# Block attention with a ternary feed-forward: chunk 5's feed-forward begun two steps sooner, a new order for chunks 6 and 7, ternary weights a step later

## The chip, the cores and the metric

One Trainium2 chip, one core. The metric is the device time of one execution in microseconds (us); the kernel before has a median of 299.28 us over three runs.

## What is computed

Input x is (2, 1024, 128) in float32. Sixteen heads of 64 attend in blocks of 16 tokens: each block of queries sees its own block, the two before it and the first token (later tokens are masked), and after the softmax the heads are mixed with a 16x16 matrix. Then comes a feed-forward of 512 hidden units with ternary weights, and a layer norm behind each of the two. Cut to what matters:

```python
qkv = xp @ w_qkv                                   # 128 -> 3 * 1024
sim = einsum('bhnid,bhnjd->bhnij', qw * scale, kw) # 16 queries x (1 + 5 * 16) keys, masked
attn = einsum('gh,bhnij->bgnij', w_th, softmax(sim))
out = concat(out_bos, einsum('bhnij,bhnjd->bhnid', attn, vw)) @ w_out + b_out
x = layernorm(x + out)

alpha = mean(abs(w)); w_t = sign(w) * (abs(w) > 0.5 * alpha)   # both weights
h = gelu((x / (rms(x) + 1e-8)) @ w_up_t.T)                     # 128 -> 512
y = (h / (rms(h) + 1e-8)) @ w_down_t.T                         # 512 -> 128
x = layernorm(x + y)
```

## The kernel before, in words

The engines' programs are written out by hand, one function for each engine, with semaphores between them; every engine works its own list in order. The 2048 tokens are 8 chunks of 256. The main loop has 32 steps, four to a chunk; a step handles four blocks of 16 queries. "s_c" below is the step a piece of data belongs to.

- `scores(s)`: 64 small matmuls and a mask on PE into bank 0. `shift(s)`: VectorE takes the maximum (L751) and subtracts it (L753). ScalarE's Exp (L632). `total(s)`: VectorE's sum (L759) and reciprocal (L761). `normalise(s)`: POOL (L448).
- Two steps later (LAG 2): `transposes` of the probabilities (L1025), which `at_hi` on ScalarE and `at_lo` on VectorE (L744) turn into the high and low part AT; `c_part` (L1064), 12 matmuls of the probabilities with windows of x; one step on, `ct_hi` on ScalarE and `ct_lo` on VectorE (L739) split its result into CTh and CTl. Float32 accuracy is had from two fp32r parts everywhere: high part, low part, and `split3` (L922 to L924) with three matmuls.
- `y_part`: 12 matmuls a step that prepare the next chunk's queries (bank 2 and 3, copied by ScalarE as Yb in `y_out`); they end with step 27. In step s%4=0 the scores wait for all Yb of their chunk.
- `o_part(n, p)`: the output projection of chunk n in four blocks of 12 matmuls, one block a step from step 4n+6 on, for chunk 6 two blocks in each of steps 30 and 31, for chunk 7 in the end.
- The feed-forward of chunk n starts at step 10+4n (F_LAG) and takes a phase k a step: k=0 `stage` (ScalarE, bias, attnS, L586), `attn_back` (PE transposes), `residual` (VectorE L767 to L778: sum, statistics), `variance_roots` (POOL L454); k=1 `up_input` (VectorE L783 to L791), `x1_T` (PE L1091), `layernorm` (VectorE L796); k=2 `x1_hi` (ScalarE), `x1_lo` (VectorE L801), `up(n,0)` (PE L1101, L1102), `gelu(n,0)` (ScalarE L603); k=3 `up(n,1)`, `gelu(n,1)`, `hidden_high` (VectorE L807, gTh), `hidden_low` (POOL L461, gTl), `squares` (POOL L467, L469), `down` (PE L1110, L1111); in the next chunk's k=0 `down_out` (ScalarE, dS), `down_back` (PE: transposes L1119 and 16 one-column sums of squares L1123), `hidden_sum` (VectorE L818), `hidden_root` (POOL L474), `second` (VectorE L823 to L841), `last_root` (POOL L480), and in its k=1 `result` (VectorE L847). Then SP stores.

A helper says which phase runs: `divmod(s - F_LAG, 4)`, one chunk at a time. So chunk 5's phases 0 and 1 fall in steps 30 and 31 and everything from its `x1_hi` on stands in the list behind the loop, mixed with chunks 6 and 7. Chunk 7's projection there comes in pieces, its last block behind `down(6)`. The weights' preparation is done in the first steps: `fills` moves data through free banks, and `ternary()` (VectorE L730, L733), four instructions of 128x512, stands at the end of step 0; its results are transposed on PE in step 2 (fill "t"). PE's step 2 begins by waiting for the copies of fill ("x", 2).

The result tile y2 is one buffer; `second(n)` waits for the store of chunk n-1.

## Time and profile before

| | us |
|---|---|
| median of 3 runs | 299.28 |
| lowest, highest | 297.99, 300.93 |
| the profiled execution | 297.8 |
| its span, first to last instruction | 295.7 |
| PE busy / VectorE / ScalarE / POOL | 235.7 / 202.6 / 143.0 / 127.0 |
| mean granted TensorE clock | 0.895 |

The span is shorter than the execution's time by 2.1 us, which lie around it. The profile covers one execution. Times in the trace count from the start of the span. PE is TensorE, DVE is VectorE, ACT is ScalarE, POOL is GpSimd; "[0.53 <-DVE x1Tl L801]" behind a row means that the engine sat idle 0.53 us before it and what ended that. PEclk is the granted clock: 1.00 is 2.4 GHz, 0.50 is 1.2 GHz.

### The profile page before, as it was taken

The numbers are of one execution on the slowest core, as the hardware profiler recorded it, in microseconds if no ns is written. First come the engines' busy times: TensorE is split into PE (matmuls) and PEld (weight loads), VectorE is DVE, ScalarE is ACT, GpSimd is POOL, SyncE is SP. The second block draws the span as 40 slices with busy tenths as digits, with TensorE's granted clock in tenths as the row PEclk, the third lists the DMA queues.
The fourth block names the chain that finished last, engine by engine and source line by source line (L and its number), as shares of the span: only waits on it lengthen the run. The fifth ranks groups of instructions, "written<-read, shape, count | busy, mean of one in ns | idle before, by whom it ended". The sixth has DMA issues, their size and how long they took to land.

```text
span 295.7 us, 9352 instructions
## 1 busy us (share of the span) xinstructions
PE 235.7 (80%) x4002; PEld 208.8 (71%) x4002; DVE 202.6 (68%) x505; ACT 143.0 (48%) x264; POOL 127.0 (43%) x148
## 2 busy tenths in 40 slices
PE   2799399989999989889988999898879745953440
PEld 2699399879898968778877888787758624952320
DVE  0757668786688669867876886698758867154631
ACT  2474246755654854595368456844742531200200
POOL 6115124134234564474457535844564162073250
PEclk9999689999999999999999999999968955867555
DMA  7635800100100200020011001000000000000000
GB/s 255 163 111 173 211 5 11 48 2 9 51 21 2 58 2 21 14 60 2 20 43 35 4 19 50 26 22 20 0 2 21 20 18 0 2 0 18 19 0 19
DMA packets 18621, 11.65 MB, mean 39 GB/s; under 512 B 2004, under 2 KB 17940, under 8 KB 18452
## 3 DMA queue, kind: packets, MB, share of 16 engines
q1 hardware_dynamic: 18000, 10.01, 11.7%
q10 hardware_dynamic: 580, 1.05, 1.2%
q8 instruction: 31, 0.51, 0.8%
q14 instruction: 10, 0.08, 0.1%
HBM read 8.91 MB, written 2.10 MB: 37 GB/s over the span
## 4 chain that ended last, share of the span: by engine, by line
DVE 39%; PE 19%; issue 16%; POOL 12%; ACT 10%; DMA 2%; POOLq 0%; DVEq 0%; ACTq 0%
DVE CTl L739 8%; DVE E L753 5%; DVE mx L751 4%; POOL gT L467 4%; DVE AT L744 4%; ACT E L632 3%; POOL gT L469 3%; DVE sm L759 3%; PE bank L922 3%; PE bank L923 2%; PE bank L924 2%; ACT L603 2%; PE bank L1064 2%; PE bank L1041 2%; POOL gTl L461 2%
## 5 line engine op out<-in xcount | busy, mean ns | idle before, releaser
L448 POOL TENSOR_TENSOR E<-E,rc 128x400 f32<-128x400 f32 x32 | 27.6, 863 | 83.1 <-DVE rc L761 83.0
L523 ACT ACTIVATE Yb<-bank 128x512 f32<-128x512 f32 x64 | 38.0, 594 | 30.6 <-PE bank L924 30.2
L739 DVE TENSOR_TENSOR CTl<-bank,CTh 128x512 fp32r<-128x512 f32 x64 | 41.1, 683 | 15.2 <-ACT CTh L523 14.9
L523 ACT ACTIVATE CTh<-bank 128x512 fp32r<-128x512 f32 x64 | 34.7, 598 | 18.3 <-PE bank L1064 18.1
L922 PE MATMUL bank<-xTh,Gh 128*128 128x256 f32 x128 | 38.3, 299 | 1.2 <-ACT Gh L523 1.2
L922 PE MATMUL bank<-CTh,Mh 128*128 128x256 f32 x128 | 37.4, 293 | 0.9 <-DVE CTl L739 0.9
L632 ACT ACTIVATE E<-E 128x400 f32<-128x400 f32 x32 | 17.2, 538 | 41.6 <-DVE E L753 41.6
L923 PE MATMUL bank<-CTl,Mh 128*128 128x256 f32 x128 | 36.9, 288 | 0.0
L924 PE MATMUL bank<-CTh,Ml 128*128 128x256 f32 x128 | 36.9, 288 | 0.0
L924 PE MATMUL bank<-xTh,Gl 128*128 128x256 f32 x128 | 36.0, 281 | 0.0
L923 PE MATMUL bank<-xTl,Gh 128*128 128x256 f32 x128 | 36.0, 281 | 0.0
L1064 PE MATMUL bank<-AT,xw 50*128 50x256 f32 x384 | 33.1, 308 | 1.5 <-DVE AT L744 1.5
L1041 PE MATMUL bank<-xT,Yb 128*32 128x50 f32 x2048 | 30.6, 214 | 1.4 <-ACT Yb L523 1.4
L1041 PEld LDWEIGHTS bank<-xT,Yb 128*32 128x32 f32 x2048 | 26.2, 113 | 7.1 <-issue 7.0
L1064 PEld LDWEIGHTS bank<-AT,xw 50*128 50x128 f32 x384 | 26.4, 197 | 6.7 <-issue 2.6
L759 DVE TENSOR_REDUCE sm<-E 128x8 f32<-128x400 f32 x32 | 18.2, 569 | 16.9 <-ACT E L632 16.9
L1025 PE MATMUL bank<-ident,E 128*128 128x128 f32 x128 | 22.4, 300 | 4.6 <-issue 4.6
L922 PEld LDWEIGHTS bank<-CTh,Mh 128*128 128x128 f32 x128 | 25.2, 197 | 1.1 <-issue 1.0
L922 PEld LDWEIGHTS bank<-xTh,Gh 128*128 128x128 f32 x128 | 24.6, 192 | 1.6 <-ACT Gh L523 1.4
L923 PEld LDWEIGHTS bank<-CTl,Mh 128*128 128x128 f32 x128 | 25.2, 197 | 0.0
L924 PEld LDWEIGHTS bank<-CTh,Ml 128*128 128x128 f32 x128 | 25.0, 195 | 0.0
L923 PEld LDWEIGHTS bank<-xTl,Gh 128*128 128x128 f32 x128 | 24.4, 191 | 0.0
(132 smaller groups left out, 512.7 us busy)
## 6 DMA issues: line engine op xcount, KB each, us to landing
raw<-in_L_attn_x SPq DMA_DIRECT2D x36, 64.0 KB
w_sb<-in_L_attn_w_qkv ACTq DMA_DIRECT2D x2, 512.0 KB, 5.2
pt_rows<-PT SPq DMA_DIRECT2D x1, 1024.0 KB, 5.8
R<-pt_rows SPq DMA_DIRECT2D x1, 1024.0 KB, 4.9
xr<-in_L_attn_x SPq DMA_DIRECT2D x6, 128.0 KB
out<-y SPq DMA_DIRECT2D x6, 128.0 KB
raw<-in_L_attn_x SPq DMA_DIRECT2D x12, 56.0 KB
xq<-in_L_attn_x SPq DMA_DIRECT2D x2, 256.0 KB, 5.3
```

The lines of the kernel that those rows point to most:

```text
L448: tt(e, e, rc[s % 2][:, :].unsqueeze(2).broadcast_to([P, TILES, WIN]), ALU.mult).then_inc(s_norm, 1)
L523: copy = lambda o, i, **k: nc.scalar.activation(o, i, ACT.Copy, **k)
L632: nc.scalar.activation(e, e, ACT.Exp).then_inc(s_exp, 1)
L739: v.tensor_tensor(ct_view(CTl[s // 4 % 2], s % 4, q), c_view(q), ct_view(f32(CTh[s // 4 % 2][:, :, :]), s % 4, q), ALU.subtract).then_inc( ...
L753: v.tensor_tensor(E[k][:, :, 0:WIN], scores, mx[k][:, :].unsqueeze(2).broadcast_to([P, TILES, WIN]), ALU.subtract).then_inc(s_sub, 1)
L759: v.tensor_reduce(sm[k][:, :], E[k][:, :, 0:WIN], AX.X, ALU.add).then_inc(s_sum, 1)
L922: mm(o, wh, rh, start=start, stop=False, **k)
L923: mm(o, wh, rl, start=False, stop=False, **k)
L924: return mm(o, wl, rh, start=False, stop=stop, **k)
L1025: ins = nc.tensor.transpose(o[:, :, IL * f:IL * f + IL], E[s % 2][:, k:k + 2, :].rearrange("p t w -> p (t w)"), ident[:, :])
L1041: mm(bank[S_BANK][lo:lo + 32, WIN * tile:WIN * tile + WIN], Yb[s // 4 % 2][:, ytile, lo:lo + 32], keys, start=(tile == 0), stop=False, ski ...
L1064: ins.append(mm(bank[C_BANK[q]][:, col], xw[s // 4 % 2][row, m, c, :], AT[row, a, col], start=(n == 0), stop=(n == 2)))
```

## The change

- Chunk 5: its projection runs two blocks each in steps 26 and 27, its feed-forward starts at step 28 in place of 30, in banks 2 and 3, which y_part has left. Steps 28 to 31 then hold phases of two chunks. Its `down` and what follows stand in the end.
- `down_back` is split: the sums of squares become `square_sum` with a semaphore of their own. For chunks 6 and 7 they go to bank 7 and take the squares of all four hidden tiles (32 one-column sums), which ScalarE computes with Square into a new tile gsq; before, POOL squared and added.
- For chunk 6, gTh is copied by ScalarE and gTl computed by VectorE (before VectorE and POOL).
- y2, mv2 and rstd2 have two buffers, each store buffer its own semaphore.
- In every step PE does `up(n,0)` behind y_part (before ahead of it) and `down(n)` behind `c_part` (before ahead); in steps s%4=3 ScalarE copies the second Yb ahead of Exp (before behind).
- `ternary()` moves to the end of step 1, and PE's step 2 waits for the copies of the last "p" fill instead of ("x", 2).
- The end behind the loop is a new list on each engine, with chunk 7's projection ahead of `up(6)` and `down(6)`; `c_part(30)` writes banks 0 and 1.

```diff
+            gsq = last.enter_context(nc.sbuf_tensor("gsq", [P, FT, CHUNK], F32))
...
         def o_parts(s):
-            if s < 30:
+            if s < 26:
                 return [divmod(s - O_LAG, 4)] if s >= O_LAG else []
-            return [(6, 2 * (s - 30)), (6, 2 * (s - 30) + 1)]
+            return {26: [(5, 0), (5, 1)], 27: [(5, 2), (5, 3)], 30: [(6, 0), (6, 1)], 31: [(6, 2), (6, 3)]}.get(s, [])
         def ffn(s):
-            return divmod(s - F_LAG, 4) if s >= F_LAG else (-1, -1)
-        UP_BANK = {5: (1, 2), 6: (2, 3), 7: (5, 6)}
-        AT_BANK = {6: 0, 7: 4}
-        DN_BANK = {6: 0, 7: 4}
+            first = [F_LAG + 4 * n for n in range(5)] + [28]
+            return [(n, s - f) for n, f in enumerate(first) if 0 <= s - f < 6]
+        UP_BANK = {5: (2, 3), 6: (0, 1), 7: (5, 6)}
+        AT_BANK = {5: 2, 6: 3, 7: 4}
+        def ss_bank(n):
+            return bank[O_BANK] if n >= 6 else dn_bank(n)
+        def c_bank(s, q):
+            return bank[q if s == 30 else C_BANK[q]]
...
 # POOL, behind the loop
-            hidden_low(5, 0)
             variance_roots(6)
-            hidden_low(5, 1)
-            squares(5, 0)
-            squares(5, 1)
             hidden_root(5)
-            hidden_low(6, 0)
-            hidden_low(6, 1)
             last_root(5)
-            squares(6, 0)
-            squares(6, 1)
+            variance_roots(7)
             hidden_root(6)
-            variance_roots(7)
+            hidden_root(7)
             last_root(6)
-            squares(7, 0)
-            squares(7, 1)
-            hidden_root(7)
             last_root(7)
...
 # ScalarE
-                need(act, f_back, n if n < 6 else n - 1)
+                need(act, f_ss, {6: 0, 7: 6}.get(n, n))
+            def hidden_high(n, t):
+                copy(gTh[n == 6][:, o, :], gT[n == 6][:, o, :]).then_inc(f_gh, 1)
+            def squares(n, t):
+                need(act, f_ss, n)
+                nc.scalar.activation(gsq[:, o, :], gT[n == 6][:, o, :], ACT.Square).then_inc(f_sum, 1)
...
                 y_out(s, 0)
+                if s % 4 == 3:
+                    y_out(s, 1)
                 nc.scalar.activation(e, e, ACT.Exp).then_inc(s_exp, 1)
-                y_out(s, 1)
+                if s % 4 < 3:
+                    y_out(s, 1)
...
 # ScalarE, behind the loop, after the change:
+ at_hi(30), ct_hi(29), stage(6), at_hi(31), ct_hi(30), down_out(5), ct_hi(31), x1_hi(6), stage(7),
+ gelu(6,0), hidden_high(6,0), gelu(6,1), hidden_high(6,1), squares(6,0), squares(6,1), down_out(6),
+ x1_hi(7), gelu(7,0), gelu(7,1), squares(7,0), squares(7,1), down_out(7)
...
 # VectorE
-                if s == 0:
+                if s == 1:
                     ternary()
...
 # VectorE, behind the loop, after the change:
+ at_lo(30), ct_lo(29), at_lo(31), ct_lo(30), ct_lo(31), residual(6), hidden_sum(5), up_input(6),
+ layernorm(6), x1_lo(6), second(5), residual(7), hidden_low(6,0), hidden_low(6,1), result(5),
+ up_input(7), hidden_sum(6), x1_lo(7), layernorm(7), hidden_high(7,0), hidden_low(7,0),
+ hidden_high(7,1), hidden_low(7,1), second(6), hidden_sum(7), second(7), result(6), result(7)
...
 # PE
                 if s == LAG:
-                    pe.wait_ge(s_eva, read_no("A", "x", 2))
-                    pe.wait_ge(s_evd, read_no("D", "x", 2))
+                    pe.wait_ge(s_eva, read_no("A", "p", 2))
+                    pe.wait_ge(s_evd, read_no("D", "p", 3))
...
 # PE, behind the loop, after the change:
+ transposes(30), c_part(30), attn_back(6), transposes(31), down(5), c_part(31), down_back(5),
+ square_sum(5), o_part(7,0), o_part(7,1), o_part(7,2), x1_T(6), o_part(7,3), up(6,0), attn_back(7),
+ up(6,1), down(6), square_sum(6), down_back(6), x1_T(7), up(7,0), up(7,1), down(7), square_sum(7),
+ down_back(7)
```

## Rows read from the trace of the kernel before

**Rows 1.** Busy time by stretch: start:end, length, each engine's us (count), PEclk, DMA share, GB/s
```profile
core 0: us, PE busy (x) PEld busy (x) DVE busy (x) ACT busy (x) POOL busy (x), PEclk, DMA share, GB/s
180.00:200.00 20.00, 18.78 (x363) 16.73 (x363) 14.83 (x41) 13.46 (x25) 11.47 (x13) 1.00 0.13 36
240.00:250.00 10.00, 2.57 (x15) 1.95 (x16) 7.41 (x12) 1.17 (x4) 6.03 (x7) 0.50 0.02 6
270.00:280.00 10.00, 2.76 (x10) 2.07 (x10) 6.42 (x28) 1.58 (x3) 1.67 (x2) 0.57 0.05 14
```
**Rows 2.** The chain that ended last: start us, us, what
```profile
core 0 of [0], span 295.7 us
...
225.12 0.12 PE bank L922
...
277.75 0.21 PE bank L1102
```
**Rows 3.** Timeline, first loop steps: start, us, engine, line, operation, [idle before, releaser]
```profile
28.14 1.55 DVE L730 TENSOR_SCALAR tern<-w_ff,tsum 128x512 f32<-128x512 f32 x2
31.06 0.57 DVE L751 TENSOR_REDUCE mx<-bank 128x8 f32<-128x400 f32 x1
...
35.37 1.08 PE L1025 MATMUL bank<-ident,E 128*128 128x128 f32 x4 [4.61 <-issue]
...
37.12 0.69 DVE L744 TENSOR_TENSOR AT<-bank,AT 128x512 fp32r<-128x512 f32 x1 [1.78 <-ACT AT L523]
38.22 0.57 DVE L751 TENSOR_REDUCE mx<-bank 128x8 f32<-128x400 f32 x1 [0.41 <-PE bank L1047]
...
40.58 0.57 DVE L759 TENSOR_REDUCE sm<-E 128x8 f32<-128x400 f32 x1 [1.18 <-ACT E L632]
...
42.77 1.29 DVE L739 TENSOR_TENSOR CTl<-bank,CTh 128x512 fp32r<-128x512 f32 x2 [0.83 <-ACT CTh L523]
```
**Rows 4.** Timeline, steps 20 to 23, where the period is 27.9 us
```profile
150.16 0.38 PE L1101 MATMUL bank<-x1Th,wuT 128*128 128x256 f32 x1 [0.53 <-DVE x1Tl L801]
...
161.07 0.38 PE L1110 MATMUL bank<-gTh,wdT 128*128 128x256 f32 x1 [0.96 <-POOL gTl L461]
...
163.37 1.29 DVE L739 TENSOR_TENSOR CTl<-bank,CTh 128x512 fp32r<-128x512 f32 x2 [1.66 <-ACT CTh L523]
...
165.44 0.16 DVE L818 TENSOR_SCALAR hss<-bank 128x2 f32<-128x2 f32 x1 [0.18 <-PE bank L1123]
...
175.31 0.54 ACT L632 ACTIVATE E<-E 128x400 f32<-128x400 f32 x1 [2.79 <-DVE E L753]
```
**Rows 5.** Timeline, steps 26 to 31 and the first table load behind them
```profile
193.45 0.56 DVE L751 TENSOR_REDUCE mx<-bank 128x8 f32<-128x400 f32 x1
...
216.43 0.39 PE L1110 MATMUL bank<-gTh,wdT 128*128 128x256 f32 x1 [2.34 <-POOL gTl L461]
...
233.25 0.57 DVE L759 TENSOR_REDUCE sm<-E 128x8 f32<-128x400 f32 x1 [0.60 <-ACT E L632]
...
235.33 1.28 ACT L603 ACT_TABLE_LOAD   x1
236.62 1.08 ACT L603 ACTIVATE gT<-bank 128x512 f32<-128x512 f32 x2
```
**Rows 6.** Timeline behind the loop
```profile
241.34 1.26 POOL L461 TENSOR_TENSOR gTl<-gT,gTh 128x512 fp32r<-128x512 f32 x1
241.40 2.21 DVE L783 SCALAR_TENSOR_TENSOR rms<-roots,eps_rms 128x1 f32<-128x1 f32 x2 [2.12 <-POOL roots L454]
...
244.44 1.82 DVE L791 TENSOR_SCALAR x1n<-res,mv,rn 128x128 f32<-128x128 f32 x2
...
247.39 0.68 DVE L744 TENSOR_TENSOR AT<-bank,AT 128x512 fp32r<-128x512 f32 x1
...
250.43 1.29 DVE L739 TENSOR_TENSOR CTl<-bank,CTh 128x512 fp32r<-128x512 f32 x2 [1.53 <-ACT CTh L523]
...
267.21 0.47 ACT L586 ACTIVATE attnS<-bank,b_sb 128x255 f32<-128x255 f32 x1 [2.18 <-PE bank L924]
...
274.10 0.35 DVE L783 SCALAR_TENSOR_TENSOR rms<-roots,eps_rms 128x1 f32<-128x1 f32 x2 [1.12 <-POOL roots L454]
...
289.46 0.60 DVE L847 TENSOR_SCALAR y<-y,mv,rstd 128x128 f32<-128x128 f32 x2 [0.81 <-POOL rstd L480]
```

More of the change, by code:

```diff
@@ L112, in attention_ffn @@
         dS = sb("dS", [P, CHUNK])
-        y2 = sb("y2", [P, CT, P])
+        y2 = [sb(f"y2_{i}", [P, CT, P]) for i in range(2)]
         st = sb("st", [P, CT, 6])
@@ L565, in ct_hi @@
                     act.wait_ge(s_C, 2 * s + 1 + q)
-                    copy(ct_view(CTh[s // 4 % 2], s % 4, q), c_view(q)).then_inc(s_CTh, 1)
+                    copy(ct_view(CTh[s // 4 % 2], s % 4, q), c_view(s, q)).then_inc(s_CTh, 1)
             def at_hi(s):
@@ L613, in _ @@
             for s in range(STEPS):
[L614 to L620 removed]
+                for n, k in ffn(s):
+                    if k == 4:
+                        down_out(n)
+                    if k == 0:
+                        stage(n)
+                    if k == 2:
+                        x1_hi(n)
                 if s == LAG + 1:
@@ L656, in _ @@
             gelu(7, 1)
+            squares(7, 0)
+            squares(7, 1)
             down_out(7)
@@ L851, in _ @@
             for s in range(STEPS):
-                n, k = ffn(s)
-                if k == 1 and n > 0:
-                    result(n - 1)
-                if k == 2:
-                    x1_lo(n)
-                if k == 3:
-                    hidden_high(n, 0)
+                for n, k in ffn(s):
+                    if k == 5:
+                        result(n)
+                    if k == 2:
+                        x1_lo(n)
+                    if k == 3:
+                        hidden_high(n, 0)
                 if s == LAG + 1:
@@ L864, in _ @@
                     at_lo(s - LAG)
-                if k == 0 and n > 0:
-                    hidden_sum(n - 1)
-                if k == 1:
-                    up_input(n)
-                if k == 3:
-                    hidden_high(n, 1)
+                for n, k in ffn(s):
+                    if k == 4:
+                        hidden_sum(n)
+                    if k == 1:
+                        up_input(n)
+                    if k == 3:
+                        hidden_high(n, 1)
                 shift(s)
-                if k == 0 and n > 0:
-                    second(n - 1)
+                for n, k in ffn(s):
+                    if k == 4:
+                        second(n)
                 total(s)
@@ L911, in _ @@
             hidden_low(7, 1)
+            second(6)
             hidden_sum(7)
             second(7)
+            result(6)
             result(7)
@@ L1135, in _ @@
                 scores(s)
-                if k == 0 and n > 0:
-                    down_back(n - 1)
-                if k == 2:
-                    up(n, 0)
-                if k == 3:
-                    up(n, 1)
+                for n, k in ffn(s):
+                    if k == 4:
+                        down_back(n)
+                        square_sum(n)
+                    if k == 3:
+                        up(n, 1)
                 if s < STEPS - 4:
@@ L1155, in _ @@
                     o_part(*part)
-                if k == 0:
-                    attn_back(n)
-                if k == 1:
-                    x1_T(n)
-                if k == 3:
-                    down(n)
+                for n, k in ffn(s):
+                    if k == 0:
+                        if n == 5:
+                            pe.wait_ge(s_Ye, 64)
+                        attn_back(n)
+                    if k == 1:
+                        x1_T(n)
                 if s >= LAG:
                     c_part(s - LAG)
+                for n, k in ffn(s):
+                    if k == 3 and n < 5:
+                        down(n)
             transposes(30)
-            pe.wait_ge(s_Ye, 64)
-            up(5, 0)
-            up(5, 1)
-            pe.wait_ge(s_sub, STEPS)
+            c_part(30)
+            pe.wait_ge(f_gelu, 12)
             attn_back(6)
-            c_part(30)
             transposes(31)
-            x1_T(6)
+            down(5)
             c_part(31)
-            down(5)
-            up(6, 0)
-            up(6, 1)
+            down_back(5)
+            square_sum(5)
             o_part(7, 0)
             o_part(7, 1)
-            down_back(5)
             o_part(7, 2)
+            x1_T(6)
+            o_part(7, 3)
+            up(6, 0)
+            attn_back(7)
+            up(6, 1)
             down(6)
-            o_part(7, 3)
+            square_sum(6)
             down_back(6)
-            pe.wait_ge(s_ATl, STEPS)
-            attn_back(7)
             x1_T(7)
@@ L1190, in _ @@
             down(7)
+            square_sum(7)
             down_back(7)
```

189 lines of the change are left out of this document (101 added, 88 removed).

## The prediction, made blind

> **What bounds the kernel now.** I read the page's first line for the span, then the table of stretches, then the chain that ended last, then each engine's timeline at four places: the first loop steps, one steady period, steps 26 to 31, and everything behind the loop. The table [rows 1] tells the two halves apart. In a steady stretch TensorE is busy 18.8 of 20 us at a granted clock of 1.00, and VectorE 14.8. Behind the loop, from 240 to 250 us, TensorE is busy 2.6 of 10 us at 0.50, and between 270 and 280 us 2.8 of 10 at 0.57, while no other engine is full. A fifth of the span [rows 2] is a serial tail: chunks 6 and 7 hand small pieces from engine to engine. So a microsecond of work matters in the loop only where a wait closes the loop, and in the tail nearly everything on the chain counts. By the chain a 256-column matmul costs 0.12 us from start to start at 2.4 GHz (clock 1.00) and 0.21 at 1.2 GHz (0.50) [rows 2].
>
> **Part 1, ternary a step later.** The four ternary instructions take 2.9 us of VectorE (28.14 to 31.1), and the maximum of step 1 starts only behind them at 31.06, though its scores were done by 28. What follows hangs on it: PE's first transposes at 35.37 had stood idle 4.61 us, the first AT waited 1.78, the first CTl starts at 42.77 [rows 3]. After the change VectorE runs the maximum at 28.2, the exponentials' sum to 30.7, the copies of xT to 32.4, the ternary work until 35.3 and then AT at once, because the transposes no longer wait for the third xT fill (only for the banks of "p") and start near 30.7. The work is the same; VectorE's waits go: 1.78 (AT), 0.41 (maximum), about 0.6 of the sum's 1.18 and 0.6 of CTl's 0.83 [rows 3]. Sum 3.4 us. Bounds: 0 if the ternary group lands on an equally tight place, 4.6 if PE's whole idle time goes. PE must wait for the ternary weights until 35.3, hidden by y_part until about 34.2. From there to step 6 the loop is a VectorE/ScalarE cycle, so I keep **-3.4**.
>
> **Part 2, order inside the steady loop.** PE's two largest waits in one period are 0.53 (x1Tl) and 0.96 (gTl) [rows 4]. The second Yb copy of a step s%4=3 now stands ahead of Exp, the first `up` behind y_part, `down` behind c_part, and the last two fill these waits. But the period is closed elsewhere: Exp, table load, Gelu, gTh, POOL's gTl and squares, `down`, dS, attnS, CTh, then CTl at 163.37 after 1.66 of idle, then VectorE nearly without gap to the next Exp [rows 4]. `down`'s second half still starts when gTl is there. What comes off this loop is 0.18 before hss (PE reaches the square sums sooner) [rows 4] and about 0.12 where c_part ended last before CTh: 0.3 a period, four periods, **-1.2**. Bounds 0 and 1.5 a period (both PE waits whole). The early Yb copy costs nothing as long as its y_part is finished: Exp stood idle 2.79 before VectorE released it [rows 4]. The two y2 buffers and their store waits remove waits that end nothing here: 0, bounds -0.3 and 0.
>
> **Part 3, chunk 5 in steps 28 to 31.** Before, the maximum of step 26 starts at 193.45 and the last sum and reciprocal end at 234.06: 40.6 us [rows 5]. Added and taken away on that stretch:
> - Steps 26 and 27 carry two blocks of chunk 5's projection each, 12 matmuls x 0.12 = 1.4 more on PE, ahead of attn_back(4) and x1_T(4). VectorE's residual comes 0.5 later: +0.5.
> - Step 29: up_input(5) enters VectorE's queue ahead of the maximum, 1.4 us undisturbed. It meets POOL's low parts and squares of chunk 4. The row for that is up_input(6): its first pair took 2.21 us while POOL's gTl ran, 0.35 for chunk 7 in quiet, and the whole group of chunk 6 ran from 241.40 to 246.26, 4.9 [rows 6]. I take the nearest in length of overlap, 1.4 + 1.9 = +3.3 (ends 1.4 and 4.9). PE waits for it in x1_T(5) with c_part(27) and down(4) behind it, and has then been idle some 6 us, where before it was 2.34 [rows 5]; the mostly idle stretch from 240 us was granted 0.50 [rows 1], so I count what follows at 1.2 GHz.
> - Steps 30, 31: residual, up_input and layernorm of chunk 5 are gone there (1.5 + 1.4 + 1.1): -4.0. Two gTh copies come in: +0.9. PE's late start, at 1.2 GHz until about 226, keeps dS, x1Th, CTh and Gelu of chunk 5 late: +1.9.
> - Gelu, Exp, Gelu now alternate once more, so two further table loads. The row shows 1.28 us, with the next Gelu directly behind it [rows 5]. One lies behind Exp(30) ahead of Gelu(5,0), one behind Gelu(5,1) and done before Exp(31) is released: 0.
>
> The sum is **+2.6**, bounds +0.5 and +8. The Trainium skill, "ScalarE: Activation LUTs", section "What ACT_TABLE_LOAD costs", counts about 2.66 us for each change of set, 1.28 of load and 1.38 of drain. The trace shows the 1.28 and no gap behind it; by the page's figure the two switches would make this part some 2.8 us dearer at most.
>
> **Part 4, the new end.** From the last reciprocal to CTl(31) complete took 17.6 us before (234.06 to 251.72), since AT(31) at 247.39 stood behind up_input(6) [rows 6]. Now VectorE has only AT and CTl first (durations of the same timeline, each unchanged in kind and rounded to 0.05): transposes 0.6, AT copy 0.65, AT low 0.65, CTl(29) 1.25, c_part(30) 0.95, attn_back 0.35, transposes 0.6, AT 0.65 and 0.7, c_part(31) 1.3 (half clock), CTh 0.7, CTl 1.25: **9.7**.
> The projection of chunk 7 follows in one piece: 19 matmuls x 0.21, 29 x 0.12 and x1_T(6) 0.4 in between: **8.0**, where before its last block waited behind down(6) and stage(7) began at 267.21, 15.5 us after CTl(31) [rows 6]. If PE stays at 1.2 GHz, 2.7 more.
> From stage(7) to the last result took 22.85 (to 290.06) [rows 6]. Now: 7.9 to the second transposes of chunk 7 (residual 1.5, then VectorE holds chunk 6's low parts until ScalarE's Gelu and copies, 5.2 after stage(7), result(5) 0.6, up_input 1.4 of which a part overlaps); 3.4 to the first Gelu; 2.4 for four split instructions of 0.44 and 0.7; half of `down` 1.0; square sums 1.2 (64 records of the kind, twice as many as before); hss 0.3, root 0.75, second 1.95, root 0.65, result 0.6. Together **20.15**. POOL's squares are gone from this chain; ScalarE's Square runs beside `down`. No row shows a Square or an SBUF copy of 128x512 on ScalarE: above 0.54 (the Exp of 400 columns [rows 4]) and below 0.60 + 1.28 if a table load is added [rows 5]. I take 0.6, nearest to the Gelu of the same shape; at 1.88 square_sum(6) would be 0.8 later, that of chunk 7 still hidden.
> The store behind the result costs 5.64 as before (290.06 to 295.7).
>
> **Sum.** 234.06 + 2.6 + 9.7 + 8.0 + 20.15 + 5.64 = 280.15; less 3.4 and 1.2 = 275.55; plus 1.0 for some thirty hand-overs of about 0.035 us that I rounded away: span 276.6. The profiled execution had 2.1 us around its span (297.8 against 295.7): 278.7. The median shown, 299.28, is 1.005 times the profiled one: **280.0 us**.
>
> **Rivals.**
> (a) Chunk 5 inside the loop costs its upper bound (+8): up_input(5) is held by POOL for all of 4.9, and PE stays at 1.2 GHz through steps 29 to 31. For: PE's idle time in step 29 grows; against: PE is then dense for 18 us. 280 + 5.4 = 285.4.
> (b) The ternary move gives nothing: the loop re-forms at another wait (x, the weights' transposes). Against: 4.61 of PE idle stands right there [rows 3]. 283.4.
> (c) The tail runs better: PE at 2.4 GHz through projection and chunk 7 (the half-clock share of the 8.0 and of the last `up`, `down` and sums is about 5): 275.
> (d) Slower than before: Yb's second copy ahead of Exp. ScalarE works in order; if y_part(s,1) ends after VectorE's subtraction, Exp, the sum, POOL's normalise and the next transposes wait. It is done in seven steps; to cancel a gain of 19 us each would have to lose over 2.8 us, on top of the 2.79 of cover in [rows 4]. At 3.0 each 21 us: 301. Only the early, PE-bound steps 3 and 7 have little cover.
>
> **How the numbers follow.** A measurement of this kernel tells about 1% (3 us) from no change. Forecast 280.0 with own range 275 to 285: 0.70. (a) 0.13, (b) 0.06, (c) 0.08, (d) 0.03. Faster by over 1% 0.95, within 1% 0.02, slower 0.03. The range takes in (a), (b) and most of (c), plus the 2.7 and 0.8 above together: 273.5 to 288.
>
> **What would show it.** Right: first CTl near 39.4; the last reciprocal near 232; CTl(31) complete about 10 us later; stage(7) about 18 after the reciprocal; last result near 270 to 271; at the end no POOL square. Wrong steps would show as up_input(5) longer than 3.5 us, a table load in front of a Square, clock 0.50 through the whole of chunk 7's projection, or Exp waiting for PE in a step s%4=3. If the last reciprocal comes later than 238, part 3 is wrong; if the stretch behind it is over 48 us, part 4 is.

## The result, and the profile after

The changed kernel took 276.71 us (median of 4 runs, 275.97 to 277.42) beside 299.0 us for the kernel before on the same chip: ratio 0.925 [0.919, 0.930]. The forecast was 280.0, range 273.5 to 288. The profiled execution took 276.39 us, its span 274.6 us. In the experiments below one execution, of the kernel with the loop order undone (281.08 us beside 275.3 to 275.5), counts as a slow one and is left out of that kernel's ratio.

The page of the kernel after: its span, and the shares of the chain that ended last.

```profile
span 274.6 us, 9482 instructions
...
DVE 39%; PE 35%; ACT 11%; issue 9%; DMA 2%; POOL 2%; POOLq 0%; DVEq 0%
```

The chain of before had POOL at 12%, "issue" at 16% and PE at 19%. POOL has left it almost wholly. Before, the chain passed through POOL's squares (1.01 and 0.74 us) in four periods from 106 to 192 us and through those of chunks 5, 6 and 7 behind; now it passes through them once, at 186.37. PE has taken the largest part of the share.

Busy time by stretch, kernel after (columns as in [rows 1]):

```profile
180.00:200.00 20.00, 19.01 (x307) 17.60 (x307) 16.05 (x46) 11.34 (x22) 11.28 (x12) 1.00 0.09 25
...
238.00:248.00 10.00, 8.72 (x91) 8.34 (x90) 5.09 (x20) 1.51 (x4) 1.69 (x2) 0.79 0.05 15
248.00:258.00 10.00, 6.47 (x93) 5.29 (x91) 6.85 (x29) 6.09 (x11) 2.40 (x3) 0.72 0.05 14
258.00:268.00 10.00, 5.86 (x82) 4.88 (x82) 6.85 (x28) 2.62 (x5) 1.85 (x3) 0.50 0.01 2
```

The loop looks as before [rows 1]. Behind it PE was busy 2.6 and 2.8 of 10 us; now 8.7, 6.5 and 5.9, with a granted clock of 0.79 and 0.72 for two of the three stretches. The serial tail has been filled in good part.

To see where the time went I use the same anchors in every trace: the start of the maximum of step k, mx(k); the end of the last reciprocal; the end of the last CTl; stage(7), that is ScalarE's attnS of chunk 7; the end of the last result. From one to the next, in us:

| leg | before | forecast | after |
|---|---|---|---|
| start to mx(0) | 25.22 | 25.22 | 26.00 |
| mx(0) to mx(10) | 57.78 | 54.4 | 54.14 |
| mx(10) to mx(26) | 110.45 | 109.25 | 108.67 |
| mx(26) to last reciprocal | 40.61 | 43.2 | 43.14 |
| to last CTl | 17.66 | 9.7 | 9.09 |
| to stage(7) | 15.49 | 8.0 | 7.80 |
| to last result | 22.85 | 20.15 | 20.03 |
| to the span's end | 5.64 | 5.64 | 5.73 |

The hand-overs of 1.0 us, which the forecast added to the whole, are in none of these legs. The columns "before" and "after" are one execution each; a repeat of the kernel after, further down, shows how far its legs can move.

**First loop steps** (timeline, kernel after), beside [rows 3]:

```profile
32.04 0.92 PE L1025 MATMUL bank<-v0T,wo_sb 128*64 128x2 f32 x26 [1.20 <-issue]
32.90 0.66 PE L1053 MATMUL bank<-ident,E 128*128 128x128 f32 x4
33.10 0.87 DVE L757 TENSOR_SCALAR tern<-w_ff,tsum 128x512 f32<-128x512 f32 x2
34.01 1.41 DVE L760 SCALAR_TENSOR_TENSOR w_ff<-w_ff,tsum,tern 128x512 f32<-128x512 f32 x2
35.34 0.68 DVE L771 TENSOR_TENSOR AT<-bank,AT 128x512 fp32r<-128x512 f32 x1
...
40.11 1.29 DVE L766 TENSOR_TENSOR CTl<-bank,CTh 128x512 fp32r<-128x512 f32 x2 [0.98 <-ACT CTh L529]
```

The transposes stood at 35.37 after 4.61 of idle [rows 3] and are now at 32.90; the ternary group (33.10 to 35.4, 2.3 us now against 2.9) runs straight into AT, whose wait of 1.78 is gone. From mx(0) to the first CTl it was 17.55 us and is 14.11.

**A steady period** (timeline, kernel after), beside [rows 4]:

```profile
159.46 1.29 DVE L766 TENSOR_TENSOR CTl<-bank,CTh 128x512 fp32r<-128x512 f32 x2 [1.61 <-ACT CTh L529]
...
160.64 0.43 PE L1160 MATMUL bank<-ones,gT 128*32 128x1 f32 x32 [1.00 <-POOL gT L484]
...
161.26 0.15 DVE L845 TENSOR_SCALAR hss<-bank 128x2 f32<-128x2 f32 x1
```

The wait of 0.18 before hss is gone, that of 1.61 before CTl is not. The new row is PE's 1.00 for POOL's squares: the transposes of dS no longer stand behind it, they ran at 159.26. The experiment on the split, below, turns on this.

**Steps 28 to 31** (timeline, kernel after), beside [rows 5]:

```profile
209.16 1.26 POOL L476 TENSOR_TENSOR gTl<-gT,gTh 128x512 fp32r<-128x512 f32 x1
210.50 1.10 POOL L482 TENSOR_TENSOR gT<-gT 128x512 f32<-128x512 f32 x1
210.63 1.12 DVE L810 SCALAR_TENSOR_TENSOR rms<-roots,eps_rms 128x1 f32<-128x1 f32 x2
...
212.46 1.51 DVE L818 TENSOR_SCALAR x1n<-res,mv,rn 128x128 f32<-128x128 f32 x2
213.89 0.56 DVE L778 TENSOR_REDUCE mx<-bank 128x8 f32<-128x400 f32 x1
214.02 0.69 PE L1122 MATMUL bank<-ident,x1n 128*128 128x128 f32 x2 [5.48 <-DVE x1n L818]
...
223.15 1.28 ACT L609 ACT_TABLE_LOAD   x1
224.44 0.60 ACT L609 ACTIVATE gT<-bank 128x512 f32<-128x512 f32 x1
...
227.62 1.28 ACT L654 ACT_TABLE_LOAD   x1
230.57 0.54 ACT L654 ACTIVATE E<-E 128x400 f32<-128x400 f32 x1 [1.67 <-DVE E L780]
```

up_input(5) lies between POOL's gTl and squares and takes 3.3 us (210.63 to 213.97) where the quiet one takes 1.4; the maximum of step 29 and PE's x1_T wait for it, PE for 5.48. Both extra table loads are there, one with Gelu 0.01 behind it, the other over before Exp was released.

**The tail** (timeline, kernel after), beside [rows 6]:

```profile
233.94 0.98 PE L1095 MATMUL bank<-AT,xw 50*128 50x256 f32 x12 [2.65 <-issue]
...
239.75 1.29 DVE L766 TENSOR_TENSOR CTl<-bank,CTh 128x512 fp32r<-128x512 f32 x2 [1.28 <-ACT CTh L529]
241.09 0.39 PE L950 MATMUL bank<-CTh,Mh 128*128 128x256 f32 x1 [1.28 <-DVE CTl L766]
...
248.84 0.47 ACT L592 ACTIVATE attnS<-bank,b_sb 128x255 f32<-128x255 f32 x1 [1.05 <-PE bank L952]
...
251.44 0.63 ACT L529 ACTIVATE gTh<-gT 128x512 fp32r<-128x512 f32 x1
...
253.12 1.13 ACT L623 ACTIVATE gsq<-gT 128x512 f32<-128x512 f32 x2
...
268.27 0.60 DVE L875 TENSOR_SCALAR y<-y,mv,rstd 128x128 f32<-128x128 f32 x2 [0.33 <-POOL rstd L495]
```

The last CTl stood at 250.43 behind up_input(6) [rows 6], now at 239.75; the projection of chunk 7 is one unbroken block from 241.09, and stage(7) comes at 248.84 in place of 267.21. Two Squares take 1.13 together and no table load stands before them.

### The profile page after: what moved, and what is told of

Same layout as the page of the kernel before. It is cut to its first block, busy times and chain, and to the rows that moved or that the text cites. A ratio compares the mean times of both kernels' runs of the same rounds, so it can differ in the third digit from the quotient of the medians.

```text
span 274.6 us, 9482 instructions
## 1 busy us (share of the span) xinstructions
PE 231.1 (84%) x4066; PEld 207.3 (75%) x4066; DVE 198.3 (72%) x505; ACT 149.8 (55%) x272; POOL 117.2 (43%) x138
## 4 chain that ended last, share of the span: by engine, by line
DVE 39%; PE 35%; ACT 11%; issue 9%; DMA 2%; POOL 2%; POOLq 0%; DVEq 0%
DVE CTl L766 9%; PE bank L950 6%; PE bank L952 5%; PE bank L951 5%; DVE AT L771 5%; PE bank L1095 4%; DVE mx L778 3%; DVE E L780 3%; DVE sm L786 2%; ACT E L654 2%; ACT L609 2%; PE bank L1069 2%; PE bank L1140 2%; DVE res L823 2%; DMA xq<-in_L_attn_x 2%
## 5 line engine op out<-in xcount | busy, mean ns | idle before, releaser
L950 PE MATMUL bank<-xTh,Gh 128*128 128x256 f32 x128 | 39.0, 305 | 1.2 <-ACT Gh L529 1.2
L1095 PE MATMUL bank<-AT,xw 50*128 50x256 f32 x384 | 32.5, 303 | 3.2 <-issue 2.7
L1095 PEld LDWEIGHTS bank<-AT,xw 50*128 50x128 f32 x384 | 25.8, 193 | 8.3 <-issue 5.2
L1069 PE MATMUL bank<-xT,Yb 128*32 128x50 f32 x2048 | 29.6, 210 | 0.0
L1069 PEld LDWEIGHTS bank<-xT,Yb 128*32 128x32 f32 x2048 | 25.1, 110 | 5.2 <-issue 5.0
L952 PEld LDWEIGHTS bank<-xTh,Gl 128*128 128x128 f32 x128 | 24.6, 192 | 0.0
```

Source lines behind the costliest of these rows:

```text
L950: mm(o, wh, rh, start=start, stop=False, **k)
L952: return mm(o, wl, rh, start=False, stop=stop, **k)
L1069: mm(bank[S_BANK][lo:lo + 32, WIN * tile:WIN * tile + WIN], Yb[s // 4 % 2][:, ytile, lo:lo + 32], keys, start=(tile == 0), stop=False, ski ...
L1095: ins.append(mm(c_bank(s, q)[:, col], xw[s // 4 % 2][row, m, c, :], AT[row, a, col], start=(n == 0), stop=(n == 2)))
```

## The experiments

Twelve runs were made (ten new kernels, and two kernels a second time), in three groups of four, each group on one chip beside the kernel before (298.23, 298.24 and 298.03 us). Every result is the median of four executions, with its ratio to the kernel before on that chip. In the third group all four first maxima came at 27.3 to 27.7 us, in the others at 25.4 to 26.1; so I compare legs, not absolute times, and medians within a group where I can.

**Part 1 alone, in the kernel before.**

```diff
-                if s == 0:
+                if s == 1:
                     ternary()
...
-                    pe.wait_ge(s_eva, read_no("A", "x", 2))
-                    pe.wait_ge(s_evd, read_no("D", "x", 2))
+                    pe.wait_ge(s_eva, read_no("A", "p", 2))
+                    pe.wait_ge(s_evd, read_no("D", "p", 3))
```

> The kernel before with one part alone: the ternary group at the end of step 1, and the first transposes waiting for the last 'p' fill. Theory (the group stood on the chain between two maxima): the maximum of step 1 starts 2.9 us sooner, the first CTl 3.4 sooner against the maximum of step 0, and all later maxima too; time 299.0 - 3.4 = 295.6 us. Rival (b) of the prediction (the chain re-forms at the weights' transposes): within 0.5 us of 299.0, and an equal wait appears in front of the first c_part.

Measured 295.0 us, 0.987 [0.981, 0.992]: 3.2 less. mx(0) to mx(10) is 54.33 (before 57.78), and every other leg is that of before (mx(10) to mx(26) 110.48, mx(26) to the last reciprocal 40.58, then 17.66, 15.6, 22.9). What the move gives is kept to the end. In the kernel after the transposes start at 32.90 and not near 30.7 as forecast, which costs nothing, since VectorE's AT stands behind the ternary group until 35.3 in any case.

**The order in the loop undone, in the kernel after.** PE does `up(n,0)` and `down(n)` at their old places, and Yb is copied behind Exp.

```diff
-                if s % 4 == 3:
-                    y_out(s, 1)
                 nc.scalar.activation(e, e, ACT.Exp).then_inc(s_exp, 1)
-                if s % 4 < 3:
-                    y_out(s, 1)
+                y_out(s, 1)
...
+                        up(n, 0)
                 (ahead of y_part; down(n) ahead of c_part likewise)
```

> The kernel after with all three changes of order in the steady loop undone (second Yb copy behind Exp in every step, up(n,0) ahead of y_part, down(n) ahead of c_part). Theory: the period of four steps goes from 27.48 back to 27.92 us, over steps 10 to 26 that is +1.8 us, and the end is as in the kernel after: 278.5 us. Rival (the 0.44 comes from the two result buffers or the split of the square sums, not from the order): the period stays 27.48 and the time 276.7.

Measured 275.4 us, 0.923 [0.921, 0.926], against 0.925 with the order: no difference. mx(10) to mx(26) is 109.23 in place of 108.67, so the order is worth 0.56 over four periods; but mx(26) to the last reciprocal is 42.37 in place of 43.14, which gives 0.77 back. Up to the last reciprocal the order brings nothing.

**Only ScalarE's order undone.** The first half of the same edit.

> The kernel after with one of the three undone: the second Yb copy behind Exp again in steps s%4=3. Theory (the copy only fills idle time of ScalarE, the period is closed by Exp, Gelu, POOL and down): period 27.48 to 27.55, time 276.7 to 277.0 us. Rival (scores of the next chunk waiting for Yb were on the loop): a wait of 0.3 us for Yb in front of the scores goes into the period in full, 7 x 0.3 = +2 us, 278.8 us.

Measured 277.6 us, 0.931 [0.927, 0.934]; mx(10) to mx(26) 108.68, the 108.67 of after. In this leg the early Yb copy costs nothing and brings nothing. The time is 2.1 us above that of the last kernel on the same chip, and the intervals don't touch. In the profiled executions the span is 2.8 us longer: 1.0 from mx(26) to the last reciprocal, 0.55 less in the leg before it, and 2.4 behind the loop, where the instruction lists of the two are the same: 11.10 and 7.77 here, 10.21 and 6.25 there (the clock, last section). So two medians of four executions can stand 2 us apart, with intervals that don't touch, for a reason that is mostly not in the edit.

**The split of the square sums undone: dS's transposes wait for the squares again.**

```diff
+                if n < 5:
+                    pe.wait_ge(f_sum, 2 * n + 2)
                 (ahead of the transposes of dS in down_back)
```

> The kernel after, and in the loop PE's transposes of dS wait for POOL's squares again before they start, as before the split of the square sums. Theory (the split, and not the order of PE's list, gave most of the shorter period, since undoing the order left 27.65 of 27.92): hss and the maximum behind it 0.3 us later in each period, from step 10 to step 26 +1.0 to +1.3 us, 277.9 us. Rival (PE now reaches this place late enough that the squares are done): no change in the period, 276.7 us.

Measured 277.8 us, 0.931 [0.924, 0.937], beside 276.5 for the kernel after in the same group; the intervals overlap, and the reading rests on the leg. mx(10) to mx(26) is 110.24, 1.57 more than after and almost the 110.45 of before; the nine profiles whose PE list is that of after up to step 26 agree there within 0.08 (108.60 to 108.68). Its timeline at the place of the rows of after above:

```profile
161.44 1.29 DVE L766 TENSOR_TENSOR CTl<-bank,CTh 128x512 fp32r<-128x512 f32 x2 [1.61 <-ACT CTh L529]
...
162.71 0.41 PE L1150 MATMUL bank<-ident,dS 128*128 128x128 f32 x2 [1.30 <-POOL gT L484]
163.05 0.43 PE L1162 MATMUL bank<-ones,gT 128*32 128x1 f32 x32
163.56 0.16 DVE L845 TENSOR_SCALAR hss<-bank 128x2 f32<-128x2 f32 x1 [0.23 <-PE bank L1162]
```

The transposes (0.34 of PE time) now lie between POOL's release and the sums, and hss waits 0.23 again. With the split they are done while PE waits for POOL anyway. So part 2's gain is mostly the split, not the order.

**Chunk 7's projection ahead of down(6), in the kernel before.** PE does the last block of the projection before `down(6)`, VectorE residual(7) and up_input(7) earlier, POOL variance_roots(7) earlier.

```diff
-            down(6)
             o_part(7, 3)
-            down_back(6)
...
+            down(6)
+            down_back(6)
```

> The kernel before with one idea of the new end alone: chunk 7's last projection block, its bias, transposes, residual and roots ahead of chunk 6's down on each engine; chunk 5 and the rest as before. Theory (the tail is a chain that begins with stage(7), and it began late only because of the order): stage(7) at about 260.5 instead of 267.2, result(7) about 7 us sooner, 292 us. Rival (what counts is chunk 5's work taken out of the end; chunks 6 and 7 only change places): no more than 2 us, 297 us or above, with second(6) or down(6) late in front of chunk 7.

Measured 294.4 us, 0.987 [0.985, 0.989]: 3.9 less, between the two expectations. stage(7) comes at 261.08 in place of 267.21, but from there to the last result it is 25.65 in place of 22.85: 2.8 are given back: chunk 7 now meets chunk 6's second half, and its input group stands beside POOL's squares of chunk 6 (the first pair 1.12 in place of 0.35, x1n 1.83 in place of 0.60). Against the kernel after, the three legs of the end come apart. The first, 17.67, is that of before: this edit leaves AT(31) and CTl(31) behind up_input(6). The second is 8.77, so the order of chunk 7's projection alone brings nearly all of its gain (15.49 to 7.80). The third is 5.6 longer than after's 20.03; the squares on POOL are 2.1 of that (the experiment on them, below), and the rest was not taken apart.

**x1_T(5) behind down(4), in the kernel after.**

```diff
-                    if k == 1:
+                    if k == 1 and n < 5:
                         x1_T(n)
...
+                if s == 29:
+                    x1_T(5)
```

> The kernel after with one line moved on PE: in step 29 the second transposes of chunk 5 stand behind c_part(27) and down(4), not ahead of them. Theory (PE's 5.5 us of idle time in step 29 hold down(4), with it dS, CTh and the maximum of step 30): down(4) ends near 214.5 instead of 218.3, VectorE's 1.5 us wait for x1Th goes and the last reciprocal comes 1.5 us or more sooner against the first maximum, 275.2 us. Rival (step 30 hangs on VectorE's own queue and on up_input(5), not on PE): the last reciprocal within 0.5 us of where it was, 276.7 us. Where TensorE's granted clock changes at another moment in the end, that alone moves the rest by up to 2 us either way, as the legs of the two kernels with the loop's order undone have shown.

Measured 276.4 us, 0.926 [0.920, 0.931]: no difference. mx(26) to the last reciprocal falls only from 43.14 to 42.66, as the rival has it. The step behind the wait is 1.4 us shorter (6.12 against 7.49), and the next is 0.9 longer (8.90 against 7.99), at a granted clock of 0.82 in place of 1.00.

**up_input(5) behind the maximum of step 29 too.** The edit above, and in VectorE's list the same one for `up_input(5)`.

> As e5_x1T5_late, and VectorE's up_input(5) in step 29 moved behind the maximum and subtraction of that step. In the kernel after this group of 1.4 us took 3.34 us (210.63 to 213.97) while POOL worked. Theory (the group, stretched by POOL, delays the maximum of step 29, and PE no longer waits for it): maximum of step 29 at 3.3 us sooner, the last reciprocal 2.5 to 3 us sooner than in the kernel after, 274 us. Rival (POOL's low part of chunk 4, ready at 213.6 in any case, ends the step): nothing beyond e5.

Measured 274.6 us, 0.919 [0.915, 0.924]. The leg is 40.61, exactly before's. mx(28) to mx(29) is 6.59 in place of 9.85: the 3.3 us of the held up_input stood on the path, and 0.7 of them come back in the next step (8.22 against 7.49). Of the leg's gain of 2.5, 2.1 return up to the last CTl (11.14 against 9.09), and the next leg is 1.6 shorter (6.25 against 7.80); the last section says why these two vary.

**Gelu(5) and what follows moved behind the loop too.** Gelu(5,0), Gelu(5,1), the high and low parts and squares of chunk 5 stand behind the loop; POOL makes the low parts there, and PE does `down(5)` behind `c_part(31)`.

```diff
-                    if k == 3:
+                    if k == 3 and n < 5:
...
+            gelu(5, 0)
+            gelu(5, 1)
```

> As e6_upin5_late, and both Gelus of chunk 5 with their gTh, gTl and squares taken out of steps 30 and 31 and put behind Exp(31); down(5) behind c_part(31). This takes out two of the table loads and two gTh copies ahead of the maximum of step 31. Theory (VectorE and ScalarE close steps 30 and 31): last reciprocal another 1 to 1.5 us sooner, chunk 7's projection starts where down(5) now ends: in all 1 us less than e6. Rival (PE's 24 matmuls a step close steps 30 and 31, and the loads are hidden): the last reciprocal no sooner, and down(5) now stands on the chain ahead of chunk 7's projection, 1 to 2 us more than e6.

Measured 273.66 us, 0.917 [0.914, 0.920]. The leg in the loop is 39.28, below before's 40.61; two table loads are gone (270 ScalarE instructions for 272), and the tail, with chunk 5's Gelu in it, is 11.67 in place of 9.09 to the last CTl, and 18.47 in place of 20.03 at the end. But the repeat of this kernel, below, has 41.42 in the same leg: 6.77 us for the step from mx(30) became 8.54, at a clock of 0.78 in place of 1.00. So whether this edit gains in the loop over the kernel of the last experiment (40.61) isn't settled; the times are 274.58 and 273.66, with intervals that overlap.

**Squares of chunks 6 and 7 on POOL again, in the kernel after.**

```diff
-            squares(6, 0)
-            squares(6, 1)
 (ScalarE; and for chunk 7 likewise)
+            squares2(6, 0)
+            squares2(6, 1)
 (POOL; and for chunk 7 likewise)
```

> The kernel after with the squares of chunks 6 and 7 on POOL again (out of gT into the same gsq tile, released by Gelu and not by gTl, all four tiles summed by PE as in the kernel after), ScalarE without Square. Theory (POOL's two squares of 1.04 us run beside VectorE's four split instructions, which they slow as up_input(5) was slowed, and end about 0.5 us later than VectorE's): the stretch from stage(7) to the last result goes from 20.03 to 21 to 22.5 us, 278.5 us. Rival (Square on ScalarE mattered only because the old squares waited for gTl; released by Gelu they are hidden): 20.0 to 20.4 us, 276.9 us.

Measured 276.75 us, 0.926 [0.922, 0.931]. In the profiled execution stage(7) to the last result is 22.17, 2.14 more than after's 20.03. The seven profiles with ScalarE's squares and this end have 19.56 to 20.03 there. The median doesn't show it (the kernel after had 276.71 and 276.48), so the size is seen in one execution only. The timeline says where the 2.14 come from (VectorE's split instructions and POOL's squares of this run):

```profile
251.61 2.48 POOL L491 TENSOR_TENSOR gsq<-gT 128x512 f32<-128x512 f32 x2 [0.65 <-ACT gT L620]
252.23 0.97 DVE L847 TENSOR_TENSOR gTl<-gT,gTh 128x512 fp32r<-128x512 f32 x1 [0.57 <-ACT gTh L540]
253.37 1.27 DVE L847 TENSOR_TENSOR gTl<-gT,gTh 128x512 fp32r<-128x512 f32 x1 [0.18 <-ACT gTh L540]
...
260.80 2.72 POOL L491 TENSOR_TENSOR gsq<-gT 128x512 f32<-128x512 f32 x2 [2.91 <-ACT gT L620]
261.22 1.41 DVE L847 TENSOR_TENSOR gTl<-gT,gTh 128x512 fp32r<-128x512 f32 x1
262.55 1.26 DVE L841 CAST gTh<-gT 128x512 fp32r<-128x512 f32 x1
```

A gTl of 0.69 takes 0.97 to 1.41 beside POOL, a gTh of 0.42 takes 1.26. ScalarE's Squares do the same work and hold nobody: beside them (260.76 to 261.90 in the kernel after) gTh took 0.42 and gTl 0.69.

**Chunk 5 from step 30, as in the kernel before; the rest as in the kernel with Gelu(5) behind the loop.** Its projection is again one block a step in steps 26 to 29, and its phases 0 and 1 fall in steps 30 and 31; x1_hi, x1_lo and both halves of `up` join the list behind the loop.

```diff
-            if s < 26:
+            if s < 30:
...
-            return {26: [(5, 0), (5, 1)], 27: [(5, 2), (5, 3)], 30: [(6, 0), (6, 1)], 31: [(6, 2), (6, 3)]}.get(s, [])
+            return {30: [(6, 0), (6, 1)], 31: [(6, 2), (6, 3)]}.get(s, [])
...
-            first = [F_LAG + 4 * n for n in range(5)] + [28]
+            first = [F_LAG + 4 * n for n in range(5)] + [30]
```

> As e7_gelu5_end, but chunk 5's feed-forward begins at step 30 as in the kernel before, its projection one block a step in steps 26 to 29, and x1Th, x1Tl, up and Gelu of chunk 5 in front of the new end. Theory (most of the gain behind step 26 is the new end; chunk 5's early start moves about as much work into steps 28 to 31 as it takes from the end, where ScalarE and VectorE idle): 1 to 3 us more than e7, 275.5 us. Rival (the early start carries the gain): 6 us more or above, 280 us, with the first transposes of the end waiting behind up(5) and Gelu, table load and two Gelus ahead of AT(31).

Measured **269.56 us, 0.903 [0.895, 0.911]**, the fastest of all: 6.9 below the kernel after (276.48) in the same group. Its four executions spread more than others, 267.23 to 271.14, and the profiled one is the slowest of them. Neither expectation had this sign: both took the early start to be a gain. Busy time by stretch of this kernel, the stretches being mx(28) to mx(29), to mx(30), to mx(31):

```profile
203.97:210.77 6.80, 5.80 (x112) 4.96 (x112) 4.96 (x10) 5.56 (x8) 3.53 (x5) 1.00 0.01 2
210.77:216.73 5.96, 3.96 (x119) 3.12 (x115) 3.87 (x9) 2.85 (x7) 4.48 (x5) 1.00 0.00 0
216.73:224.13 7.40, 7.40 (x124) 6.85 (x124) 7.07 (x26) 2.12 (x4) 3.30 (x4) 1.00 0.13 39
```

The same three stretches of the kernel after:

```profile
204.04:213.89 9.85, 3.29 (x85) 2.59 (x85) 8.97 (x24) 5.66 (x8) 6.47 (x7) 0.88 0.05 14
213.89:221.38 7.49, 7.36 (x133) 6.39 (x134) 5.22 (x12) 2.67 (x6) 2.59 (x3) 0.70 0.02 4
221.38:229.37 7.99, 7.99 (x129) 7.49 (x129) 7.68 (x22) 5.79 (x8) 4.72 (x6) 1.00 0.06 18
```

And of the kernel before:

```profile
207.68:214.49 6.81, 5.61 (x106) 4.80 (x104) 4.97 (x10) 5.56 (x8) 3.54 (x5) 1.00 0.00 0
214.49:222.84 8.35, 6.41 (x120) 5.16 (x121) 3.87 (x9) 3.03 (x7) 4.46 (x5) 0.64 0.01 2
222.84:231.47 8.63, 8.63 (x130) 8.09 (x131) 8.22 (x32) 2.12 (x4) 3.30 (x4) 0.96 0.12 35
```

And of the kernel with Gelu(5) behind the loop (its repeat in the same group), the one from which only the start of chunk 5 differs:

```profile
204.22:210.81 6.59, 3.75 (x89) 3.06 (x91) 5.81 (x17) 5.34 (x8) 3.54 (x5) 0.89 0.07 20
210.81:219.31 8.50, 7.78 (x126) 6.33 (x125) 7.82 (x19) 3.09 (x7) 5.51 (x6) 0.50 0.01 3
219.31:227.85 8.54, 8.54 (x118) 8.03 (x119) 6.43 (x20) 2.12 (x4) 2.26 (x3) 0.78 0.07 19
```

In step 28 VectorE is busy 8.97 of 9.85 us in the kernel after, with chunk 5 in it, and 4.96 of 6.80 in this one; but this difference was already gone with up_input(5) behind the maximum (6.59). What the start at step 30 brings beyond that lies in step 29: there up_input(5) and the layer norm of chunk 5 keep VectorE busy 7.82 of 8.50 us, and 3.87 of 5.96 without them. In the same step the kernel after has a clock of 0.70, the kernel before 0.64, the kernel with Gelu(5) behind the loop 0.50, and only this one keeps 1.00 through all three stretches. How much of the 2.5 us in step 29 is VectorE's work and how much the clock, these runs don't separate. Steps 26 and 27 give another 1.0 (14.23 against 15.23, with 13.11 against 14.82 of PE time). In sum mx(26) to the last reciprocal is 37.57, against 43.14 after and 40.61 before. And the tail, which now holds the whole second half of chunk 5, is hardly longer: 9.82, 8.29 and 18.20 us, together 36.31, against 9.09, 7.80 and 20.03, together 36.92, in the first profile of the kernel after, and 34.87 in its second. Its timeline shows why; ScalarE's and VectorE's waits for c_part and the transposes take it in:

```profile
229.52 1.28 ACT L613 ACT_TABLE_LOAD   x1
230.81 1.09 ACT L613 ACTIVATE gT<-bank 128x512 f32<-128x512 f32 x2
...
235.84 1.29 DVE L773 TENSOR_TENSOR CTl<-bank,CTh 128x512 fp32r<-128x512 f32 x2 [1.18 <-ACT CTh L533]
```

VectorE had stood idle 2.75 us at this place in the kernel after (before the AT at 236.58), and ScalarE 2.69 before the AT it splits.

**The kernel after, and the kernel with Gelu(5) behind the loop, once more,** in that same group, so that the comparison doesn't go across chips. No edit.

> The kernel after, unchanged, beside the others on one chip. All theories: 276.7 us. Theory on the granted clock: from the first maximum to that of step 26 the trace is the same as in the first profile within 0.3 us, or 1.0 us shorter where the clock does not fall after the start; the legs behind the last reciprocal differ by up to 2 us with the place at which the clock changes. Rival (the legs are fixed by the list): every leg within 0.3 us.

> The kernel of e7_gelu5_end, unchanged, beside the kernel after on one chip. Theory (the three moves in steps 29 to 31 are worth about 3 us, of which a later projection of chunk 7 gives a part back): 273.7 us, 3 us or 1.1 per cent below the kernel after. Rival (the difference seen so far is the spread between chips and runs): within 1 us of the kernel after.

Measured 276.48 us, 0.926 [0.920, 0.931], and 274.54 us, 0.921 [0.915, 0.926]. The repeat of the kernel after has 162.28 us from mx(0) to mx(26) (162.81 in the first profile), 43.10 to the last reciprocal (43.14), and 9.07, 6.24 and 19.56 in the tail, together 34.87 against 36.92. So its legs aren't fixed by the list. The step from 276.48 to 274.54 (the three moves of chunk 5's pieces in steps 29 to 31) is small, about 2, with intervals that overlap; the step from 274.54 to 269.56 (where chunk 5 starts, the only difference) is 5.0, with intervals that don't touch. In the two profiles it is 1.0 in steps 26 and 27, 2.5 in step 29, 1.1 in step 30 (where 1.8 separate the two profiles of the one kernel) and 1.8 in the tail, less 1.5 in the other legs. Two other kernels stood 2.1 us apart without a cause in their lists, so the sign of the 5.0 is shown, its size to about 2 us.

## Why the prediction was right, and where not

**Right in the whole.** The predicted span was 276.6, the measured one 274.6. By the table: the part up to mx(26) came out at 4.64 less, as forecast (4.6), but by two errors that cancel (0.24 and 0.58 more gain than forecast in the first ten and the next sixteen steps, against a start 0.78 later). The rest is -0.06 in steps 26 to 31, -0.6, -0.2 and -0.1 in the tail, and the 1.0 of hand-overs. That last one was a term without a row, and no leg shows it. The close fit in the tail is partly luck: I had forecast 37.85 for its three legs together, this profile has 36.92, and the repeat of the same kernel 34.87. What lies around the span was 1.8, not 2.1, and the median was 1.001, not 1.005 times the profiled execution; together 1.3 more.

**Part 1** held in mechanism and size: -3.4 forecast, 3.44 to the first CTl, 3.2 in the time of the kernel that has this alone. Rival (b), that the move gives nothing, is out.

**Part 2: the size near, the cause wrong.** I gave 0.3 a period to the order, by "PE reaches the square sums sooner" and c_part before CTh. Measured are 0.44 a period, of which the order has 0.14 and the split 0.39 (each was undone alone, so the two need not add up). The order did what I said of `up` and `down` in it, it filled waits that end nothing. What I read over is that `down_back` was one function with one wait in front: the transposes of dS stood behind POOL's squares, though they need only dS. The row was there, hss with its 0.18 [rows 4], and the chain of before passed through POOL's squares in each of these periods; I looked at when PE arrives, and not at what PE does between the release and hss.

**Part 3: size and steps right, the question not asked.** +2.6 forecast, +2.53 measured: 1.0 in steps 26 and 27 (0.5 forecast), 3.04 in step 28 to 29 (3.3), then -0.86 and -0.64. up_input(5) at 3.34 us was the 3.3 taken from [rows 6]. PE was back at a clock of 1.00 by 221.4, and not about 226. Rival (a), +8, is out. Of the two table loads one was over before Exp was released; the other ended 0.01 us ahead of Gelu, which may have waited for it, so my 0 is shown for the first alone. The Trainium skill, "ScalarE: Activation LUTs", section "What ACT_TABLE_LOAD costs", counts 2.66 us for a switch of set with 1.38 of it as drain; here the load of 1.28 has the next Gelu 0.01 us behind it, so the trace doesn't show a drain of this size. Taking both loads away, together with what hung on them, gave a leg of 39.28 us in one profile and 41.42 in the next, against 40.61, so no price of the loads can be read from it. But I priced the part only as a cost inside the loop and booked all of part 4's gain without asking how much of it needs part 3. The kernel with chunk 5 from step 30 answers: little or none. Against it the kernel after is 5.5 or 5.6 us longer between mx(26) and the last reciprocal, and its tail is 0.6 longer in one profile and 1.4 shorter in the other (36.92 and 34.87 against 36.31); the early start alone costs 5.0 in the medians.

**Part 4** held: the last CTl at 9.09 (9.7), stage(7) at 7.80 (8.0), the last result at 20.03 (20.15). The 8.0 counts 19 of the 48 matmuls at half clock; the profile had some 15 of them so, the repeat took 6.24 at 1.00, and six of the eight profiles with this list took 6.2 to 6.3. The term was 1.7 too dear for these. For Square on ScalarE I had taken 0.6: two took 1.13, with no load before them; the SBUF copy took 0.63. The gain of 19 us is 8.6, 7.7 and 2.8 in the three legs. The second is the order's, by the experiment on chunk 7's projection. The third needs POOL relieved: with the order alone the leg grew by 2.8, and with the squares back on POOL it is 2.1 longer. The first, AT and CTl of step 31 ahead of up_input(6), was not tested alone; the timelines before and after show only that the place where they stood is gone. Nor was gTl of chunk 6 on VectorE, or the new place of c_part(30), tested alone. Rival (c), the tail at full clock, held for the projection in six of eight profiles, where it is worth 1.6 us, and not for chunk 7: the last 10 us before the last result ran at 0.50 in all fourteen profiles.

**Rival (d)**, Yb ahead of Exp as a loss, is out with a gain of 22 us; undone alone it leaves mx(10) to mx(26) at 108.68 against 108.67.

## What to carry to other kernels

Before work is brought forward out of a serial tail, look whether the tail has idle time for it on each engine that it uses, and whether the loop has: here the tail did, and the loop did not. The kernel with chunk 5 back at step 30 is 2.5% faster than the change, and 1.8% faster than the kernel from which it differs in this alone. Where one wait guards two pieces of work, see which of them needs it. And a small instruction of VectorE that works from SBUF alone, beside a long one of POOL, is not to be priced by its quiet row: here the pair of 0.35 us took 1.12.

## What the runs showed of the hardware

**Small VectorE instructions beside POOL.** The pair of one-column instructions L810 took 0.35 us in quiet and 1.12 beside POOL's squares of 1.10; x1n 0.60 and 1.51; gTl 0.69 and up to 1.41. CTl, one of whose inputs is a bank, took 1.27 to 1.29 everywhere (two instructions), and the maximum, which reads a bank alone, 0.56 or 0.57, in steps with and without POOL work. The Trainium skill, "SBUF — State Buffer", section "Who interferes with whom", says that a VectorE instruction with two SBUF inputs contends with a GpSimd instruction that reads SBUF, that one in a two-port mode contends too, and whoever issues first then holds the shared pair for its whole instruction, and that one with at most one SBUF input outside those modes doesn't. The traces agree in which instructions are held. The pair of L810 began 0.13 us behind POOL's squares and ended 0.15 behind them (211.75 against 211.60).

**The same list, another clock.** The kernel after and its second run have the same instructions, but from the last CTl to stage(7) one took 7.80 us and the other 6.24. The granted clock from 244 to 248 us was 0.80 in the first; in the second:

```profile
240.00:244.00 4.00, 2.86 (x51) 2.56 (x52) 2.65 (x10) 1.06 (x2) 0.62 (x1) 0.98 0.08 21
244.00:248.00 4.00, 4.00 (x36) 4.00 (x36) 2.61 (x12) 0.39 (x1) 1.07 (x2) 1.00 0.06 15
```

Over the eight runs with this list between the last CTl and stage(7) the leg was 6.2 to 6.3 six times and 7.8 twice. From the last reciprocal to the last result the seven with one list there took 34.58 to 38.90 us. c_part(30), behind a wait of 2.65, took 0.98 us in the kernel after and 1.65 in the one with the loop order undone. In this tail, where PE is idle and busy by turns, one profiled execution can't settle a question of 2 us or even 4. Nor can it in the last steps of the loop, where one kernel had 39.28 and 41.42. The leg from mx(10) to mx(26), at a clock of 1.00 throughout, can: 108.60 to 108.68 in nine profiles.

**PE's idle time seems to be paid twice.** In step 29 PE was busy 6.41 us with 120 matmuls at a clock of 0.64 in the kernel before, 7.36 with 133 at 0.70 in the kernel after, and 3.96 with 119 at 1.00 in the kernel with chunk 5 from step 30. The two lower clocks stand behind idle times of 2.34 [rows 5] and 5.48 us, the full one behind waits of 1.00 at most. That the idle time brings the lower clock is read from these rows, and no run varied it alone; in the two profiles of the kernel with Gelu(5) behind the loop the same wait of 1.63 had c_part(27) behind it once at 0.97 us and once at 1.65. I had counted the clock in part 3, but not seen that the end of before's own loop paid for it too, and so was not the best that could be had.
